# Re-spacing the filler work of a planned attention kernel: shorter prologues, no extra room behind inverses, two products kept in one piece

## What is computed

```python
# layer 1, "squared": q and k through a feature map, squared causal scores instead of a softmax
q = layer_norm((h @ Wq.T) * gamma + beta) * D**-0.5; k = layer_norm((h @ Wk.T) * gamma + beta)
attn = where(tril, (q @ k.T) ** 2, 0); o = (attn @ v) / (sum(attn) + EPS); return o @ Wo.T
# layers 2 and 4, "gated": per token one head's key and value are chosen by a gate, all heads share them
k_shared = sum(indicator * k); v_shared = sum(indicator * softmax_top1 * v)
att = softmax(where(tril, q @ k_shared.T * D**-0.5, -inf)); y = att @ v_shared
# layer 3, "mqa": one key head and one value head for all queries, causal softmax, output projection with bias
```

## Time and profile before

| | us |
|---|---|
| device time, median of 3 runs | 4017.52 (4014.93 to 4022.45) |
| device time of the profiled execution | 4020.66 |
| its span, first to last instruction | 4018.9 |
| TensorE busy | 3647.1 (91%) |
| GpSimd busy | 2982.7 (74%) |
| VectorE busy | 2170.1 (54%) |
| ScalarE busy | 1624.3 (40%) |
| mean granted TensorE clock | 0.977 of 2.4 GHz |

### The profile page before, as it was taken

How to read it: one execution, slowest core, us unless ns; L and a number is a source line. 1 busy time by engine, 2 the same in 40 slices (tenths; PEclk the granted TensorE clock), 3 DMA queues, 4 the chain that set the end, 5 groups by cost and what they waited for, 6 DMA issues and landing times.

```text
span 4018.9 us, 66697 instructions
## 1 busy us (share of the span) xinstructions
PE 3647.1 (91%) x25570; PEld 1450.4 (36%) x25570; DVE 2170.1 (54%) x5132; ACT 1624.3 (40%) x2433; POOL 2982.7 (74%) x2207
## 2 busy tenths in 40 slices
PE   8899999997989999999888888888998999999976
PEld 5343534432333333333333333333333333333332
DVE  1222323233556766666666656565665666676663
ACT  1554545554043333434444434343332334343343
POOL 3988788896067767777888877787667677776786
PEclk9999999998999999999999999999999999999997
DMA  2000101020110010100101010010101001010011
GB/s 74 27 6 27 38 16 48 6 70 33 45 33 1 32 32 1 64 1 25 40 13 53 6 48 12 30 35 17 48 1 35 30 1 64 1 54 1 1 43 32
DMA packets 63286, 115.02 MB, mean 29 GB/s; under 512 B 8576, under 2 KB 9088, under 8 KB 62976
## 3 DMA queue, kind: packets, MB, share of 16 engines
q1 hardware_dynamic: 62976, 110.75, 8.5%
HBM read 77.17 MB, written 33.55 MB: 28 GB/s over the span
## 4 chain that ended last, share of the span: by engine, by line
PE 54%; DVE 7%; ACT 6%; issue 4%; POOL 3%; DMA 0%; POOLq 0%; SPq 0%; DVEq 0%; ACTq 0%
PE banks L1181 11%; PE banks L1134 11%; PE banks L1166 9%; PE banks L1228 8%; PE banks L1127 7%; ACT probs_soft L870 5%; PE banks L1163 3%; DVE banks L966 3%; PE banks L1327 3%; DVE maxima_soft L961 2%; POOL added_soft L781 2%; PE banks L1195 1%; DVE rest_soft L1085 1%; DVE maxima_soft L966 1%; PE banks L1325 0%
## 5 line engine op out<-in xcount | busy, mean ns | idle before, releaser
L870 ACT ACTIVATE probs_soft<-banks 128x1024 f32<-128x1024 f32 (+1 forms) x960 | 848.4, 936 | 1195.1 <-PE banks L1166 1171.2
L781 POOL TENSOR_TENSOR added_soft<-added_soft,probs_soft 128x512 f32<-128x512 f32 (+1 forms) x380 | 1153.0, 3034 | 21.3 <-POOL added_soft L774 6.4
L966 DVE CUSTOM_DVE_ANT_0 banks<-banks,mask 128x128 f32<-128x128 f32 (+3 forms) x1536 | 701.3, 528 | 516.5 <-PE banks L1181 516.0
L961 DVE TENSOR_REDUCE maxima_soft<-banks 128x2 f32<-128x1024 f32 x384 | 452.6, 1221 | 367.5 <-PE banks L1181 367.4
L1181 PE MATMUL banks<-k_soft,q_soft 32*128 32x512 f32 (+3 forms) x4608 | 499.7, 525 | 77.6 <-ACT probs_soft L870 77.4
L876 ACT ACTIVATE probs_squared<-banks,key_scale_squared 128x512 f32<-128x512 f32 (+3 forms) x768 | 379.7, 590 | 341.5 <-PE banks L1166 337.1
L1127 PE MATMUL banks<-xnT,wide 128*128 128x512 f32 x1024 | 509.9, 620 | 5.0 <-DVE rest_soft L1085 1.9
L1134 PE MATMUL banks<-wide,xnT 128*128 128x512 f32 x1024 | 497.0, 613 | 1.0 <-ACT q_soft L853 1.0
L1166 PE MATMUL banks<-q_soft,k_soft 32*128 32x512 f32 (+3 forms) x4608 | 476.0, 495 | 0.0
L758 POOL TENSOR_SCALAR_AFFINE_SELECT probs_soft<-probs_soft 128x512 f32<-128x512 f32 x384 | 239.4, 637 | 313.8 <-ACT probs_soft L870 308.3
L1228 PE MATMUL banks<-probs_soft,v_soft 128*32 128x512 f32 (+3 forms) x4608 | 438.3, 499 | 20.2 <-ACT q_soft L855 4.8
(11 more groups left out here) (136 smaller groups left out, 4075.7 us busy)
## 6 DMA issues: line engine op xcount, KB each, us to landing
tiles<-out SPq DMA_DIRECT2D x96, 256.0 KB, 2.7
rest_soft<-out SPq DMA_DIRECT2D x96, 256.0 KB, 2.9
out<-rest_soft SPq DMA_DIRECT2D x96, 256.0 KB, 2.1
tiles<-in_x SPq DMA_DIRECT2D x32, 256.0 KB, 2.7
rest_squared<-in_x SPq DMA_DIRECT2D x32, 256.0 KB, 2.8
out<-rest_squared SPq DMA_DIRECT2D x32, 256.0 KB, 2.0
wide<-in_gated_wqkvT SPq DMA_DIRECT2D x3, 1024.0 KB, 7.6
probs_squared<-in_squared_wk SPq DMA_DIRECT2D x1, 1024.0 KB, 5.5
```

What stands on the lines that cost most here:

```text
L781: ins = pool.tensor_tensor(sums, sums, slot(ph, n)[:, :, col:col + width], ALU.add)
L870: ins = act.activation(slot(ph, n)[:, 2 * a:2 * a + 2, 0:width], score_pair(e, a)[:, :, 0:width], ACT.Exp, scale=SCALE)
L961: ins = dve.reduce_max(m["maxima"][:, ph % 2, 2 * a:2 * a + 2, t, p], score_pair(e, a)[:, :, col:col + width], AX_X)
L966: ins = dve.tensor_tensor_reduce(scores, scores, k["mask"][:, CHUNK - width:CHUNK], 1.0, MASKED, ALU.add, ALU.max, m["maxima"][:, ph % 2, ...
```

## The change

It has five parts. (1) `VALUES_IN` says how many of the four pieces of `av` go into the half of `VALUES_AT` and how many into the next: C was 2 and 2 and is 4 and 0 (half 1), A was 2 and 2 and is 0 and 4 (half 9), B stays at 2 and 2. (2) In a half with `av` no filler is placed unless it is due by then. (3) `INVERTED`, 0.85 of room for each `inv`, is gone. (4) The prologue of the second act leaves the last two `vall` to phase 0 (due by half 6), and `q` of phase 1, second chunk, goes from ahead of `kt` to between the rows bursts. (5) The prologue of the first act leaves the features of phase 1 to phase 0 (due by half 18) and the four `v2` of the second pair of head groups to phases 0 to 2 (due by half 44).

```diff
+VALUES_IN = {"C": (4, 0), "A": (0, 4), "B": (2, 2)}
-INVERTED = 0.85
@@ keys_and_values
+        if s == 0:
+            return [("gt", s, 0)], first + [("krep", s, 1), queries[1][0], ("kt", s, 0), ("kt", s, 1)], \
+                [queries[1][1]] + [("vall", s, t) for t in range(NT)]
@@ phase
-        at[h] += [("more", ("av", of, part))] * 2
-        at[h + 1] += [("more", ("av", of, part)), ("av", of, part)]
+        values = [("more", ("av", of, part))] * (PIECES["av"] - 1) + [("av", of, part)]
+        at[h] += values[:VALUES_IN[part][0]]
+        at[h + 1] += values[VALUES_IN[part][0]:]
...
-            if event[0] == "inv":
-                room[first + later] += INVERTED
@@ since
+    if event[0] == "v2" and event[1] == 0 or event[0] in ("q2", "k2") and event[1] < NG:
+        return 0
@@ spread
-        while (x := due(queue, n)) is not None and (least * weight(queue[x][0], kinds) <= room or queue[x][2] <= n + 1):
+        alone = any(e[0] == "av" or e[0] == "more" and e[1][0] == "av" for e in h)
+        while (x := due(queue, n)) is not None and (not alone or queue[x][2] <= n + 1) and (least * weight(queue[x][0], kinds) <= room or queue[x][2] <= n + 1):
@@ plan
-        events += between + first
+        values = [e for e in between + first if e[0] == "v2"]
+        events += [e for e in values if e[2] == 0] + [e for e in first if e[0] != "v2"]
+        behind_first = [(in_pieces(rest, kinds), HALVES - 2), (in_pieces([e for e in values if e[2]], kinds), 2 * HALVES + 4)]
     if soft:
         rows = [("rows", 0, k) for k in range(NRB)]
+        behind_first = [(in_pieces(rest[len(rows) - 2:], kinds), 6)]
+        rest = rest[:len(rows) - 2]
...
-    else:
-        events += rest
...
+        if s == 0:
+            work = work[:1] + behind_first + work[1:]
```

## The result

The changed kernel takes 3928.55 us (median of 4 runs, 3928.49 to 3932.66) against 4018.23 (4014.93 to 4022.45) for the one before, a ratio of 0.9779 [0.9762, 0.9796]: 90 us less by the medians, 89 by the ratio. I forecast 3966 within 3930 to 4008.

The account below looks back on a forecast made before the run. TensorE, busy 91%, plus what it waits for, was taken to bound the kernel. 4020.7 - 18 - 3 - 29 - 2 = 3968.7, stated as 3966 against the median 4017.5; range 3930 to 4008, held at 0.8.

Parts of the forecast that it names:

- rooms and inverses: Second act: INVERTED removed; 20 sparse phases net 0 with the bunches, bounds +14 and -20; inverses cost nothing.
- First prologue: First act's prologue and first batch: 29.5 us of TensorE work moves into phases 0 to 2; -18 us, bounds +1 and -24.
- Second prologue: Second act's prologue: two vall, 7.3 us, move to phase 0, about 2 us of waits added; -3 us, bounds 0 and -6.
- Bunches: Second act's 28 full phases: waits of 0.51 and 1.03 us go, 43 us in all, two thirds taken; -29 us.
- some holes will open elsewhere: Full phases of the second act: new waits, for one behind keys burst 4; only two thirds of 43 us taken.
- Rest of the first act: First act's other phases, same bunches but nothing scored in odd halves: -2 us, bounds +8 and -8.
- Only the prologues pay: Whole kernel: waits removed behind rows burst 4 and keys burst 1 reopen elsewhere; 3994 us, chance 0.25.
- GpSimd binds the first batch: First act's first batch: masks behind adds keep TensorE waiting, first term becomes -5; 3979 us, chance 0.13.
- The inverses come into the open: Halves 11 to 17: two of four rows bursts wait 0.92 us for VectorE's inverses, +87; 4053 us, chance 0.12.
- Nothing moves: Whole kernel: bunches overshoot in sparse phases (+14), first batch gives 5, holes reopen; within 8 us of 4017, chance 0.08.
- The port: First batch: moved GpSimd work could lengthen VectorE's L1076 by at most 4.3 us, once or twice a phase; sum left unchanged.

Follow-up runs that it names:

- The light kernels: Kernels before and after, each with second-act row maxima over 32 columns, inverses over 1 and the exponent scaled down: 3884.85 and 3855.23 us.
- the split in the last stage: Kernel after, with A and C split 2 and 2 and filler allowed beside av in the second act's last stage only: 3926.63 us, 0.9774.

## Why the prediction was right in direction and short by 38 us

**The step that failed** is the one on rooms and inverses: "Rooms without inverses spread the filler over the halves that wait instead; I take -0.7 a phase for it, which no row shows; net 0", and behind it "So VectorE keeps slack everywhere and I cost this at nothing". Its size is -49 us alone. The 19.8 us of VectorE in 26.3 us (75%, 80% forecast) in the halves from 11 on is right, and so is slack as an average; the conclusion was not. What the runs showed in its place: the room behind inverses draws filler into halves where VectorE comes to the bank last, and TensorE waits up to 2.9 us for it. Put in last, on top of bunches and prologues, the same edit is worth 83 us. Windows of halves 11 to 19 after, in phase 7:

```profile
1541.93:1568.20 26.27, 26.10 (x172) 8.84 (x172) 19.78 (x29) 11.21 (x15) 23.19 (x10) 1.00 0.00 1
```

I checked whether VectorE could do its work in the time of nine halves, not whether it had emptied a bank when the third piece of one half came. And I read phase 7, where the filler is a gated stage's, for all 28 full phases. The stages that gained 45 are those whose `out` is the long projection of the mqa layer (L1327, four pieces). In the other stages behind stage 0 it is one short piece (L1325), with the same eight additions on VectorE a stage. Why the long one matters so much was not varied.

Term by term, in one order: rooms -49 for 0; bunches, the first act's included, -18 for -31; prologues -22 for -21. So the prologues' term came out in size, and the bunches' term was too large by 13 us, which hid a part of what the rooms' term lacked.

**First prologue.** Forecast -18, with -29.5 + 11.5. The profile has -29.4 + 12.8. The idle time (9.4 against a forecast 9.3), the clock (0.99 for 0.98) and the missing long waits came as said. GpSimd is busy 86% of the 200 us from phase 0 on (90% from 100 to 300 us), where I said 89%: it did not bind. The time by runs is less sharp: about 10 of the prologues' 22.

**Second prologue.** Forecast -3, bounds 0 and -6. The second of the bare rows bursts waits 1.50 us and keys burst 0 behind it 1.58, 3.1 together where I said 3.9:

```profile
1078.82 1.14 PE L1191 MATMUL banks<-k_soft,q_soft 32*128 32x512 f32 x8 [1.50 <-DVE maxima_soft L971]
1081.54 0.40 PE L1173 MATMUL banks<-shift_soft,ones 32*128 32x512 bf16 x4 [1.58 <-DVE maxima_soft L976]
```

By the profile 3.7 won, by the runs 12. The sum of both prologues, -21, was measured as -22 on top of the rest, and as -6 with the old rooms: work moved into stage 0 costs 9.5 us there when the halves that take it are the wrong ones, and -3.2 with the bunches and the new rooms.

**Bunches.** Forecast -29 in the 28 full phases. The 0.51 and 1.03 us went as the text said. Alone, the full stages (0 to 2 and 7 to 10) sum to -13 in the profile, the other 20 phases to +15.8, where I took +14 with -14 from the rooms beside it, and the first act with both prologues to +5. On top of the rooms the full stages gain 21 more and the others lose 7: -18 by the runs. So "some holes will open elsewhere", for which I took a third, was a half with the new rooms (21 of 43 us won in the full stages) and over two thirds with the old ones (13 of 43). The planner's lists show where the filler goes that the bunches' halves held: with the old rooms mostly behind keys bursts 1, 4 and 8 (halves 2, 8 and 16), not behind masked rows bursts. Why that costs more with the old rooms is open; no run takes it apart.

**Rest of the first act.** Forecast -2 with bounds of 8; its stretches up to phase 14 sum to +2.2.

**The rivals.** "Only the prologues pay": refuted, they are worth 22 of 90. "GpSimd binds the first batch": refuted by the idle time. "The inverses come into the open": refuted, cutting them changes the kernel after by less than 1 us. What it got half right is the mechanism, a rows burst's VectorE work followed by an inverse. It was at work before, holding up the filler's bank as well as the next burst, and the change took it away. "Nothing moves": refuted. The range missed the time by 1.5 us, because its lower end held no gain from the rooms beyond the sparse phases.

**What stays open.** The light kernels still differ by 31 us, and by the profiles the prologues and the stages beside them make only about half of it; no run takes the rest apart. Why the stages with the long `out` gain most isn't shown. The split of the 22 between the prologues isn't settled. That a third work bank would do what the rooms do wasn't tried.

## What to carry to other kernels

A planner's room is a claim about one engine: put into it only what that engine is really free for, and ask of each piece placed there who empties its bank and what stands ahead of that in the other engine's queue; the busy share of that engine over a phase doesn't answer it. When a change has parts that share one budget of slots, try the rooms first, and then the rest on top: alone, two of the three parts here looked worthless, and with the first one right they gave 40 us. For a blind estimate, read one phase of every kind of stage, not one phase for all.

## What the hardware showed that I had not expected

**The clock behind a wait.** Busy time by stretch, before, around the wait of 9.57 us in the earlier trace rows:

```profile
190.00:200.00 10.00, 1.64 (x16) 0.44 (x12) 5.25 (x2) 5.40 (x12) 10.00 (x6) 0.72 0.00 0
200.00:205.00 5.00, 1.89 (x12) 0.68 (x16) 0.00 (x0) 0.00 (x0) 5.00 (x3) 0.50 0.00 0
205.00:210.00 5.00, 5.00 (x48) 2.60 (x41) 0.69 (x1) 1.64 (x5) 4.92 (x4) 0.70 0.00 0
210.00:215.00 5.00, 5.00 (x34) 3.10 (x32) 0.69 (x1) 3.55 (x9) 3.50 (x6) 1.00 0.03 5
```

TensorE is at 1.2 GHz while it hardly works and for some time behind. Short waits do it too: after the two of 1.50 and 1.58 us above, in the kernel after,

```profile
1075.00:1081.50 6.50, 3.45 (x23) 1.15 (x21) 5.26 (x10) 0.60 (x1) 0.00 (x0) 1.00 0.00 0
1081.50:1085.00 3.50, 3.46 (x14) 1.40 (x15) 1.37 (x5) 1.33 (x2) 0.00 (x0) 0.54 0.00 0
1085.00:1090.00 5.00, 5.00 (x25) 1.97 (x24) 2.53 (x15) 0.60 (x1) 1.80 (x6) 0.98 0.01 3
```

the same eight records of L1176 take 1.89 us (from 1081.75) that take 1.03 at the full clock in phase 7, above. Over the whole kernel this is the 20 us or so of busy time in the result.

**The same order, not the same time.** Between profiles of kernels whose stages have one and the same order, a stage differs by up to 7.7 us in 212 (stage 4: -3.9 in the kernel after, +1.3 with the old second prologue, +3.8 with the split in the last stage), and the first stage of the first act by anything from +12.8 to +17.2 over before. The stage table of single profiles is good for the 45 us above, not for 8; so the -4.5 us of the last stage's split can't be read from it either.

**The port.** VectorE's product with both inputs in SBUF, which I had weighed against the moved GpSimd work, did not get longer. One line's duration in ns, min/median/max, after:

```profile
L1086 DVE TENSOR_TENSOR y_squared<-y_squared,sums_squared x31: 691/1761/3715, 119.3 to 952.2; 128x512 f32<-128x512 f32 x31
```

against the earlier trace rows. The spread over the same shape is still there, and the traces say where it comes from. Two of these instructions in the kernel before, the first begun while GpSimd was in one of its additions, the second while GpSimd did nothing:

```profile
339.41 4.51 POOL L774 TENSOR_TENSOR added_squared<-probs_squared 128x2048 f32<-128x2048 f32 x1
342.72 1.75 DVE L1076 TENSOR_TENSOR y_squared<-y_squared,sums_squared 128x512 f32<-128x512 f32 x1
...
411.67 0.69 DVE L1076 TENSOR_TENSOR y_squared<-y_squared,sums_squared 128x512 f32<-128x512 f32 x1
```

The first ends 0.55 us after GpSimd's addition (343.92 to 344.47). So it is with 27 of the 31 before: they begin during an addition (L774 or L781) and end 0.55 us after it, whatever was left of it; the other four take 0.69. After, it is 22 of 31, which is why the median fell. The product waits for GpSimd's instruction to end and then runs. The Trainium skill (SBUF — State Buffer, section Who interferes with whom) accounts for it by the port that VectorE and GpSimd share, and the trace agrees.
